# Making the first tile's q and all of k once for all heads, and placing their parts through DRAM

## The reference

```
qkv = layer_norm(x, g1, be1) @ w_qkv          # 4096 x 3 x 8 x 16
scores = einsum('nhd,mhd->hnm', q, k) * 0.25
scores = where(adj != 0, scores, -inf)
attn = softmax(scores); out = einsum('hnm,mhd->nhd', attn, v)
x = x + out @ w_proj + b_proj
x = x + gelu(layer_norm(x, g2, be2) @ w1 + b1) @ w2 + b2
```

## Time and profile before

| | us |
|---|---|
| median of 3 runs (1699.94 to 1702.98) | 1702.24 |
| the profiled execution, its own time | 1704.14 |
| its span | 1702.3 |
| PE busy in the span | 1588.7 (93%) |
| DVE busy | 1419.3 (83%) |
| ACT busy | 1274.2 (75%) |
| POOL busy | 1167.4 (69%) |
| DMA from SP's queue, share of 16 engines | 26.7% |
| DMA from ACT's queue, share of 16 engines | 3.3% |

### The profile page before, as it was taken

One profiled execution on the slowest core, in us unless ns is written; L12 is line 12 of the kernel. 1 busy time (PEld: TensorE's weight loads), 2 busy tenths in 40 slices (PEclk: granted clock), 3 DMA queues, 4 the chain that ended last, 5 costly groups with the idle time before them and its releaser, 6 DMA issues.

```text
span 1702.3 us, 46524 instructions
## 1 busy us (share of the span) xinstructions
PE 1588.7 (93%) x17016; PEld 496.5 (29%) x17016; DVE 1419.3 (83%) x4490; ACT 1274.2 (75%) x1394; POOL 1167.4 (69%) x1092
## 2 busy tenths in 40 slices
PE   6989999999999999999999999999999999999996
PEld 3422222323223232232323232232323232232323
DVE  6888989987999889997898879998899879988811
ACT  4647878777777878778776877778787787868793
POOL 4955487569865798568875698567885688657551
PEclk9979999999999999999999999999999999999997
DMA  8810046301460046500462025700464015600000
GB/s 214 184 52 2 5 142 128 76 5 57 141 124 30 5 116 138 97 5 26 137 127 63 5 81 136 134 2 5 133 130 88 4 39 148 123 18 5 14 5 13
DMA packets 177856, 125.88 MB, mean 74 GB/s; under 512 B 140974, under 2 KB 155183, under 8 KB 177628
## 3 DMA queue, kind: packets, MB, share of 16 engines
q1 hardware_dynamic: 163196, 108.49, 26.7%
q10 hardware_dynamic: 14432, 14.42, 3.3%
HBM read 77.25 MB, written 6.04 MB: 49 GB/s over the span
## 4 chain that ended last, share of the span: by engine, by line
PE 52%; ACT 22%; issue 14%; POOL 8%; DVE 2%; ACTq 1%; DMA 1%; SPq 0%; POOLq 0%; DVEq 0%
ACT probs L820 20%; PE pv_ps L1149 15%; PE ring_ps L1080 10%; PE score_ps L1241 9%; PE score_ps L1256 9%; POOL probs L582 2%; PE ring_ps L1207 2%; PE score_ps L1173 2%; POOL k_stack L543 2%; ACT q_stack L689 1%; DVE masked_out L858 1%; PE ring_ps L1198 1%; PE ring_ps L1183 1%; PE ring_ps L1190 1%; POOL row_mask L517 1%
## 5 line engine op out<-in xcount | busy, mean ns | idle before, releaser
L858 DVE CUSTOM_DVE_ANT_0 masked_out<-ring_ps,row_mask 128x512 bf16<-128x512 f32 x2048 | 1311.9, 688 | 138.6 <-PE ring_ps L1080 99.3
L820 ACT ACTIVATE probs<-score_ps,score_scale 128x1024 f32<-128x1024 f32 x1010 | 1075.6, 1112 | 338.5 <-PE score_ps L1256 324.4
L582 POOL TENSOR_TENSOR probs<-probs,keep 128x1024 int32<-128x1024 int32 x256 | 604.2, 2361 | 252.1 <-ACT probs L820 241.6
L1149 PE MATMUL pv_ps<-probs,v_ones 128*17 128x512 f32 x4096 | 543.7, 599 | 4.6 <-POOL probs L582 4.0
L1080 PE MATMUL ring_ps<-k_stack,q_stack 51*64 51x512 f16 x4096 | 488.0, 397 | 15.1 <-DVE row_max L858 13.8
L1256 PE MATMUL score_ps<-q_stack,k_stack 51*64 51x512 f16 x4040 | 370.4, 391 | 18.9
L1080 PEld LDWEIGHTS ring_ps<-k_stack,q_stack 51*64 51x64 f16 x4096 | 169.0, 104 | 495.7 <-DVE row_max L858 446.2
L1241 PE MATMUL score_ps<-mask_t,ident_bf 64*64 64x512 bf16 x3028 | 274.9, 387 | 34.1 <-ACT probs L820 15.5
L1256 PEld LDWEIGHTS score_ps<-q_stack,k_stack 51*64 51x64 f16 x4040 | 115.6, 104 | 211.6 <-PE score_ps L1241 183.6
L858 DVE DVE_READ_ACCUMULATOR2_ANT row_max<- 128x1 f32 x2048 | 169.9, 83 | 0.0
L521 POOL TENSOR_SCALAR row_mask<-row_mask 128x1024 bf16<-128x1024 bf16 x124 | 129.5, 1045 | 23.6 <-POOL row_mask L517 23.0
(11 more groups left out here) (128 smaller groups left out, 840.3 us busy)
## 6 DMA issues: line engine op xcount, KB each, us to landing
adj_in<-adj SPq DMA_DIRECT2D x128, 512.0 KB, 4.2
halves<-attn ACTq DMA_DIRECT2D x30, 128.0 KB, 2.7
q_stack<-q_dram SPq DMA_DIRECT2D x42, 64.0 KB
mask_t<-row_mask SPq DMA_TRANSPOSE x128, 3.5
xq<-xnT_dram ACTq DMA_DIRECT2D x8, 256.0 KB, 2.7
halves<-halves ACTq DMA_DIRECT2D x16, 128.0 KB, 2.2
x_res<-x ACTq DMA_DIRECT2D x8, 256.0 KB, 4.5
out<-rows ACTq DMA_DIRECT2D x8, 256.0 KB, 5.4
```

Source lines behind the costliest of these rows:

```text
L582: nc.gpsimd.tensor_tensor(view, view, keep[:, KEPT.index(m), :].unsqueeze(1).broadcast_to([128, 2, TILE]), ALU.mult).then_inc(probs_masked, 1)
L820: nc.scalar.activation(probs[:, (2 * g + n) % SLOTS, :], score_banks(i, place).rearrange("p a n -> p (a n)"), ACT.Exp, scale=score_scale[: ...
L858: nc.vector.tensor_tensor_reduce(out=masked_out[:, place % 3, :], in0=ring_ps[:, place % 3, :], in1=row_mask[:, j, ch * 512:(ch + 1) * 512 ...
L1149: last = nc.tensor.matmul(pv_ps[32 * k:32 * k + HD + 1, :], v_ones[:, block_of(g, b), 2 * p + a, :], probs[:, (2 * g + b) % SLOTS, a * TIL ...
```

## The change

Instead of 36 items there are 9: item 0 is the first tile's q for all heads (with `wq_all`), items 1 to 8 are k of one chunk for all heads (with `wk_all`). For each, ACT copies the PSUM result as float16 (the high part) and as float32; POOL subtracts, which gives the low part. ACT then stores both parts to DRAM (`store_item`), waits until they are there, and loads them into the stacks' partitions (`load_item`): 6 DMAs for q, 9 for each chunk of k. These loads stand in ACT's list in the chunk after the one that stored them. The constant rows of `k_stack` are set once by DVE in pair 0, chunk 0, and spread over the other 31 pair-chunks by two DMAs of ACT at the very start. DVE also clears the shift rows of both q stacks (4 memsets instead of 2). The two clearings and six DVE scalings of the repeated weights go. POOL converts two mask blocks after each of items 1 to 6. The steps stay 4 for each chunk (`FIRST_PER`), and the row units follow 8 steps behind instead of 7.

Diff, cut to its core:

```diff
-ITEMS = PAIRS * (1 + CHUNKS)
+FIRST_PER = 4
+ITEMS = 1 + CHUNKS
 DEPTH = 4
-ROW_LAG = 7
+ROW_LAG = 8
-POOL_FIRST_MASKS = {4 + 2 * k: 4 + k for k in range(CONVERTED - 4)}
+POOL_FIRST_MASKS = {n: (2 * n + 2, 2 * n + 3) for n in range(1, 7)}
...
+        item_dram = nc.dram_tensor("item_dram", (ITEMS, 2, DIM, 512), F16, kind="Internal").ap()
...
             for n in range(ITEMS):
-                if blk > 0:
-                    again = slice(128 * 2 + 64, 128 * 3)
-                    nc.gpsimd.tensor_tensor(k_stack[:, p, blk - 1, 0:K_FIRST], item_x[n % DEPTH][:, again],
-                                            item_neg[n % DEPTH][:, again], ALU.add)
-                nc.gpsimd.tensor_tensor(dst, item_x[n % DEPTH], item_neg[n % DEPTH], ALU.add).then_inc(item_done, 1)
+                nc.gpsimd.tensor_tensor(item_part[n % DEPTH][1], item_x[n % DEPTH], item_part[n % DEPTH][0],
+                                        ALU.subtract).then_inc(item_done, 1)
...
+            def take_item(n):
+                act.wait_ge(item_full, n + 1)
+                if n >= DEPTH:
+                    act.wait_ge(item_stored[n - DEPTH], 32)
+                nc.scalar.copy(item_part[n % DEPTH][0], score_ps[:, n % 4, :])
+                nc.scalar.copy(item_x[n % DEPTH], score_ps[:, n % 4, :]).then_inc(item_read, 1)
+            def store_item(n):
+                act.wait_ge(item_done, n + 1)
+                for low in range(2):
+                    act.dma_start(item_dram[n, low], item_part[n % DEPTH][low]).then_inc(item_stored[n], 16)
+            def load_item(n):
+                act.wait_ge(item_stored[n], 32)
+                for m, first in enumerate(PART_ROW):
+                    low = Q_LOW[m] if n == 0 else K_LOW[m]
+                    heads = item_dram[n, low].rearrange("(p a d) n -> a d p n", a=2, d=HD)
+                    for a in range(2):
+                        rows = slice(HALF * a + first, HALF * a + first + HD)
+                        to = q_stack[0][rows, :, :] if n == 0 else k_stack[rows, :, n - 1, K_FIRST:]
+                        act.dma_start(to, heads[a]).then_inc(item_in[n], 16)
+                    if n > 0:
+                        act.dma_start(k_stack[rows, :, n - 1, 0:K_FIRST],
+                                      heads[1][:, :, 128 * 2 + 64:128 * 3]).then_inc(item_in[n], 16)
...
+            for c in range(CHUNKS):
+                transposed_rows(c)
+                if c == 1:
+                    load_item(0)
+                if c >= 1:
+                    load_item(c)
+                if c + 1 < CHUNKS:
+                    root(c + 1)
+                if c == 0:
+                    take_item(0)
+                take_item(c + 1)
+                act.wait_ge(stage_full, 2 * c + 2)
+                nc.scalar.copy(v_ones[...], pv_ps[...]).then_inc(v_done, 1)
+                if c == 0:
+                    store_item(0)
+                store_item(c + 1)
+            load_item(CHUNKS)
...
             for a in range(2):
-                nc.vector.memset(q_stack[1][HALF * a + SHIFT_ROW:HALF * (a + 1), :, :], 0.0).then_inc(q_clear, 1)
+                nc.vector.memset(k_stack[HALF * a + SHIFT_ROW:HALF * (a + 1), 0, 0, :], SHIFT_UNIT).then_inc(unit_set, 1)
+                for stack in q_stack:
+                    nc.vector.memset(stack[HALF * a + SHIFT_ROW:HALF * (a + 1), :, :], 0.0).then_inc(q_clear, 1)
...
+                if p == 1 and blk < CHUNKS:
+                    pe.wait_ge(xnT_ready, blk + 1)
+                    for n in ((0, 1) if blk == 0 else (blk + 1,)):
+                        if n >= 4:
+                            pe.wait_ge(item_read, n - 3)
+                        nc.tensor.matmul(score_ps[:, n % 4, :], wq_all[:, :] if n == 0 else wk_all, xnT[blk % 4],
+                                         start=True, stop=True).then_inc(item_full, 1)
                 if st >= ROW_LAG:
-                    pe.wait_ge(item_done, PAIRS * (ch + 1) + 1)
+                    if j == 0:
+                        pe.wait_ge(item_in[ch + 1], 16 * (3 * len(PART_ROW)))
```

More of the change, by code:

```diff
@@ L219 @@
 K_CHUNK = K_FIRST + 512
-ITEMS = PAIRS * (1 + CHUNKS)
+FIRST_PER = 4
+ITEMS = 1 + CHUNKS
 DEPTH = 4
-ROW_LAG = 7
-FIRST_STEPS = PAIRS * CHUNKS + ROW_LAG
+ROW_LAG = 8
+FIRST_STEPS = FIRST_PER * CHUNKS + ROW_LAG
 DVE_MASKS = {1: 2, 2: 3}
-POOL_FIRST_MASKS = {4 + 2 * k: 4 + k for k in range(CONVERTED - 4)}
+POOL_FIRST_MASKS = {n: (2 * n + 2, 2 * n + 3) for n in range(1, 7)}
 def row_unit(g, x):
@@ L312, in program @@
         wqkv = probs[:, 5, 0:3 * DIM]
-        wq_rep = probs[:, 5, 3 * DIM:3 * DIM + PAIRS * 128].rearrange("p (q r) -> p q r", r=128)
         xn_rows = [rows2[:, :, :], x_res[:, :, :]]
         xnT = [attn[:, 0, :], attn[:, 1, :], halves[:, 0, :], halves[:, 1, :]]
-        item_neg = [hidden[:, n // 2, 256 * (n % 2):256 * (n % 2) + 256].bitcast(F16) for n in range(DEPTH)]
+        item_part = [[hidden[:, 2 * low + n // 2, 256 * (n % 2):256 * (n % 2) + 256].bitcast(F16) for low in range(2)]
+                     for n in range(DEPTH)]
         item_x = [probs[:, 6 + n // 2, TILE * (n % 2):TILE * (n % 2) + TILE] for n in range(DEPTH)]
@@ L328, in program @@
         item_full, item_read, item_done = sem("item_full"), sem("item_read"), sem("item_done")
+        item_stored, item_in = ([sem(f"item_stored{n}") for n in range(ITEMS)], [sem(f"item_in{n}") for n in range(ITEMS)])
+        unit_in = sem("unit_in")
         shift_full, shift_stored = sem("shift_full"), sem("shift_stored")
@@ L706, in _ @@
+            act.wait_ge(unit_set, 2)
+            for a in range(2):
+                own = k_stack[HALF * a + SHIFT_ROW:HALF * a + SHIFT_ROW + SHIFT_PARTS + 1, :, :, :]\
+                    .rearrange("r p c k -> r (p c) k")
+                act.dma_start(own[:, 1:, :], own[:, 0:1, :].broadcast_to([SHIFT_PARTS + 1, PAIRS * CHUNKS - 1, K_CHUNK]))\
+                  .then_inc(unit_in, 16)
             root(0)
-            act.wait_ge(q_clear, 2)
+            act.wait_ge(q_clear, 4)
             act.wait_ge(w_in, 16 * 5)
-            act.wait_ge(consts_in, 16 * 4)
+            act.wait_ge(consts_in, 16 * 3)
@@ L710, in _ @@
             act.wait_ge(v_ones_set, 1)
[L711 to L728 removed]
+            for c in range(CHUNKS):
[5 more added lines that the diff above has]
+                if c + 1 < CHUNKS:
+                    root(c + 1)
+                if c == 0:
+                    take_item(0)
+                take_item(c + 1)
+                act.wait_ge(stage_full, 2 * c + 2)
+                nc.scalar.copy(v_ones[:, c * SUB:(c + 1) * SUB, :, 0:HD],
+                               pv_ps[:, :].rearrange("p (s h d) -> p s h d", s=SUB, h=HEADS)).then_inc(v_done, 1)
+                if c == 0:
+                    store_item(0)
+                store_item(c + 1)
@@ L1293, in constants @@
         c[32 * k + HD, 128 + k] = 1.0
-    for r in range(128):
-        for n, first in enumerate(PART_ROW):
-            if first <= r % HALF < first + HD:
-                c[r, 132] = -Q_LOW[n]
-                c[r, 133] = -K_LOW[n]
-        if SHIFT_ROW <= r % HALF < SHIFT_ROW + SHIFT_PARTS:
-            c[r, 135] = SHIFT_UNIT
     return c
```

62 lines of the change are left out of this document (17 added, 45 removed).

## The result

| | before | changed |
|---|---|---|
| median, us | 1702.05 (4 runs, 1699.94 to 1702.98) | 1730.66 (4 runs, 1730.08 to 1731.64) |
| profiled execution, its span | 1704.14, 1702.3 | 1730.11, 1728.2 |
| DVE's clearing behind the 64 units | 104.58 | 134.54 |
| first matmul of the loop | 117.67 | 147.65 |

The changed kernel is slower: ratio 1.017, 95% interval 1.0153 to 1.0188, that is +28.6 us on the medians. I had forecast +15. The whole difference lies ahead of the loop: its first matmul comes 30.0 us later. From there to the end the profiled executions take 1584.6 and 1580.6 us. So I follow the start phase.

What follows compares the result with a forecast made beforehand. POOL was taken to bound the start phase; ACT's serial round of 10.7 us, taken as 11.2, would replace it, ending the row units at 119.4 instead of 104.5: +15 us, 1717 us, range 1708 to 1726 (8 in 10: 1701 to 1732).

Steps and rivals of the forecast that it cites:

- Sign and mechanism: Start phase: ACT's serial stores, waits and loads replace POOL as the pace; slower by 15 us, loop itself unchanged.
- choking DMA queues: Rival, start phase: stores take 5.5 us, loads 0.58 each, so 13.6 us a chunk, +34 us; from +24 on, chance 0.13.
- chunk 1 starts: Start phase: chunk 1 begins at about 26.0 us, behind six memsets, adjacency blocks and their masks.
- chunk 1 lasts: Start phase: chunk 1 holds both q and k loads and takes 11.4 us, so chunk 2 starts at 37.4.
- six rounds, to the last stores issued: Start phase: six more chunks of 11.2 us each, ending at 104.6 us.
- last item and last units: End of the row units: last store lands, nine loads land by 114.1 us, then PE's last eight units take 5.3.
- rows end: End of the 64 row units of pair 0: 119.4 us instead of 104.5, +15 us.
- The round: ACT's list, each chunk: landing 3.8, loads 4.15, root 0.2, copies 0.9, POOL 1.2, store 0.46: 10.7 us, taken as 11.2.
- The DMA engines: Start phase: 832 more packets at 52 ns add 2.7 us a chunk, making 11.0 to 11.7 us of DMA work.
- The lag: Row units: ROW_LAG 8, one step more, moves no wait and costs nothing, since PE waits for the loads anyway.
- Cold PE: Rival, start phase: PE's clock falls to 0.50, some 0.4 us more a chunk, +18 us in all; chance 0.15.
- even case: Rival, start phase: quick stores give rounds of 8.7 to 9.5 us, time within 3.4 us of now; chance 0.09.

Runs made afterwards that it cites:

- runs with idle matmuls: Matmuls with unread results added to keep PE busy: on all edits together 1711.26 us, only from chunk 2 1703.44, on the changed kernel alone 1735.23.
- all edits together: Changed kernel with spreading DMAs after the first stores, loads a chunk later, ROW_LAG 12, repeated columns by POOL, transposes behind the last item: 1712.72 us, ratio 1.0063.
- lag 11: All edits together plus idle matmuls from chunk 2 on, one in each place, with ROW_LAG 11 instead of 12: 1710.82 us, ratio 1.0052.
- transposes behind: Changed kernel with SyncE issuing the mask transposes only when the last item's loads have landed: 1722.25 us, ratio 1.0116.

## Why the prediction was right, and where not

**Sign and mechanism.** Right: with POOL relieved, ACT's chain of stores, waits and loads sets the start phase, nothing in the loop moves, and the loop starts late by as much as the row units do. The chain of waits and the windows show it as forecast. The size was half of what came. The result, +28.6, lies outside the forecast's own range (+6 to +24) and inside the wide one by 1.3 us only, which is luck rather than reckoning. It lies where I had put the choking DMA queues (from +24 on, chance 0.13), though their price came up in another way than by 13.6 a round.

**The sum, term by term.** Forecast and profile agree at one place only, the end:

| term | forecast | measured | difference |
|---|---|---|---|
| chunk 1 starts | 26.0 | 30.7 | +4.7 |
| chunk 1 lasts | 11.4 | 14.6 | +3.2 |
| six rounds, to the last stores issued | 67.2 | 75.6 (45.3 to 120.9) | +8.4 |
| last item and last units | 14.8 | 13.6 (120.9 to 134.5) | -1.2 |
| rows end | 119.4 | 134.5 | +15.1 |

- *Chunk 1's start* is the edit I costed at nothing, "the two spreading DMAs at ACT's start are out 20 us ahead of the first unit". True of their own landing, wrong of what they pass: the second adjacency block, which chunk 1 waits for. Removing them from there gave back 4.5 of its 5.3 us (16.79 before, 22.08, 17.59).
- *Chunk 1's length*: the six q loads were issued in 2.93 us as reckoned, but the stores before them took from 27.14 to 33.66 to be issued and land, at a share of 1.14, where a later and quieter pair takes 2.5.
- *The round*: from the first store to the first load 4.7 us on average (forecast 4.3; single rounds 2.5 to 8.7), nine loads 4.9 with the gap to the root (forecast 4.15; 0.45 each in quiet rounds, 0.6 in full ones), root to stores 3.1 (2.3). The last is the copy of v, which ACT's list has ahead of the stores: I had it "within POOL's subtraction", but it waits for PE, 9.5 us in five rounds, and PE for loads and at half clock. In three of the six rounds ACT waits 1.1 to 6.6 us for the stores to land; in the others 0.4 or less, since it has already waited 1.3 to 2.1 us for PE's transposes ahead of them. The parts make 12.6 against 10.7; the 0.5 I had added for the DMA engines was too little by 1.4.
- *The DMA engines* are the step that failed. I worked out 11.0 to 11.7 us of their work for a chunk and then took 11.2 for the round, as if a full engine only fills the gaps of the one beside it. ACT's chain waits for landings, so at full load the two add up: with the transposes away the same list runs in 10.9. That this is near the 10.7 of the sum is chance: its first term is 1.0 shorter there (3.3, not 4.3), its last 0.8 longer (3.1, not 2.3), with PE at half clock. The estimate of the work itself was fair: in us 45.28 to 120.93, the six rounds, the share is 0.95, so 12.0 us of all engines a round by the same measure. It had 52 ns of an engine for each packet; in us 0 to 130 ACT's queue shows 0.306 x 130 x 16 / 10176 = 63 ns:

```profile
q10 hardware_dynamic: 10176, 8.41, 30.6%
```

- *The lag* of one step "moves no wait": right in kind. PE does wait for the loads (13.3 us in six waits), and more lag only adds at the end.
- *Cold PE*: it held as I described it, 0.50 from the start phase into the loop, but as an addition in the changed kernel it can't be told from zero; when DMA no longer bounds it is worth 2.3 us a round (10.8 to 8.5), 7 to 9 us in all. The round of 10.76 looks like the bound of 10.8 us a chunk "just under P", but PE's busy time in it is 9.8 us; the rest is waiting.
- *A slip in the even case*: from 11.2 down to 8.7 it is 2.5 us a round, not 2.0. It would move that case's low end to 1.5 us faster than now, still within its 3.4.
- Forecast for the changed profile: rounds every 11 (12.6), a load holds ACT 0.45 to 0.6 (yes), stores land in 3 to 5 us (3.7), share over 0.9 (over 1.1), POOL half busy (yes), loop start about 133 (147.7).

**What stays open.** The parts do not add up to one account: the start is worth about 8 us and the transposes about 8, but removing one alone moves the load elsewhere, as the spreading DMAs did. Which DMA engine is full at which time is not in the profile. Whether their small packets are why the transposes cost so much was not tried.

## What to carry to other kernels

When work moves from an engine to DMAs, sum what the DMA engines already carry in that stage, and if the sum comes near the stage's length, price every landing on the serial chain at its loaded value, not at the quiet one: here 6.0 instead of 2.5 us for the same loads. A DMA that is "out long before it is needed" still costs what it delays; look for the next transfer in flight that somebody waits for. And when the engines' work is thinned out, check what clock is left: PE's row matmuls went from 400 to 631 ns, and a round in which PE has about 5.8 us of work at full clock (my estimate ahead of the runs with idle matmuls) took 10.8.

## What the runs showed of the hardware that I had not expected

- Two DMAs of 104.6 KB from three partitions each held up a 512 KB load by 4.5 us.
- A DVE scaling of 128x256 took 7.13 us beside a POOL memset, 0.35 without.
- PE busy 9.21 of 10 us stayed at 0.50 (all edits together), while the kernel before stood at 1.00 with 8.72 of 9.5 busy; with two more matmuls a round the last rounds ran at 1.00 (row matmuls of 400 ns), but with lag 11 one window of them fell back to 0.66 (us 70 to 80).
- The packets of sixteen transposes of 256 KB and two adjacency loads add up to 26.7 us of all 16 DMA engines (transposes behind).
- The clock column can mislead: in the kernel with the transposes behind it reads 1.00, while its row matmuls last 631 ns, as they do elsewhere at 0.50:

```profile
50.00:60.00 10.00, 9.06 (x42) 4.50 (x36) 7.28 (x27) 2.53 (x5) 5.44 (x6) 1.00 0.77 209
```
```profile
L1105 PE MATMUL ring_ps<-k_stack,q_stack 51*64 51x512 f16 x44 | 10.5, 631 | 1.4 <-DVE row_max L887 1.2
```

Of that kernel's four runs one reads a mean clock of 0.995 and three 0.956 or 0.957, at the same times (1722.1, and 1720.8 to 1723.6).
